# Last feed forward: the second batch's normalized rows made on GpSimd and turned ahead of its low-rank products

## What is computed

```python
h = layernorm(x) * (1 + cb) + sb
logits = h @ gate_w.T + gate_b                  # 8 experts
top_v, top_i = top_k(softmax(logits), 2)
for e in range(8):
    gate = (top_i == e).sum(-1) * top_v.sum(-1)
    inter = h @ wi.T + bi + (h @ lora_A[e].T) @ lora_B[e].T   # 512 wide, rank 16
    out += gate * (relu(inter) @ wo.T + bo)
x = x + gb * out
```

## Time and profile before

| | us |
|---|---|
| median of 3 runs | 973.53 (973.2 to 974.91) |
| the profiled execution | 973.75 |
| its span, first to last instruction | 972.0 |
| TensorE busy | 909.9 (94%) |
| ScalarE busy | 642.2 (66%) |
| VectorE busy | 593.1 (61%) |
| GpSimd busy | 292.5 (30%) |

### The profile page before, as it was taken

How to read it: one execution, slowest core, us unless ns; L and a number is a source line. 1 busy time by engine, 2 the same in 40 slices (tenths; PEclk the granted TensorE clock), 3 DMA queues, 4 the chain that set the end, 5 groups by cost and what they waited for, 6 DMA issues and landing times. The chain is left out here.

```text
span 972.0 us, 25390 instructions
## 1 busy us (share of the span) xinstructions
PE 909.9 (94%) x10211; PEld 668.2 (69%) x10211; DVE 593.1 (61%) x1355; ACT 642.2 (66%) x1094; POOL 292.5 (30%) x367
## 2 busy tenths in 40 slices
PE   7998897369999999999999999999999999998987
PEld 6676576146777767777776777777677777776776
DVE  5556111566666666666666666666666666677975
ACT  2552143158787878778787878778787877884442
POOL 5124800503224242422324142232414223215110
PEclk9998799569999999999999999999999999999999
DMA  8300701100020002002000200100020010000000
GB/s 251 137 2 22 254 26 52 40 1 2 2 90 3 2 2 92 2 2 84 9 3 1 91 2 2 76 17 2 2 91 1 3 31 10 3 1 2 1 23 22
DMA packets 27128, 35.48 MB, mean 37 GB/s; under 512 B 6042, under 2 KB 21716, under 8 KB 26836
## 3 DMA queue, kind: packets, MB, share of 16 engines
q1 hardware_dynamic: 25988, 31.76, 10.0%
q0 software_dynamic: 1024, 2.10, 0.7%
HBM read 28.48 MB, written 5.37 MB: 35 GB/s over the span
## 5 line engine op out<-in xcount | busy, mean ns | idle before, releaser
L552 DVE CUSTOM_DVE_ANT_0 soft<-SC,strips 128x1024 f32<-128x1024 f32 x256 | 303.3, 1223 | 79.7 <-PE SC L394 79.6
L513 ACT ACTIVATE soft<-soft,nmax 128x1024 f32<-128x1024 f32 x256 | 294.1, 1150 | 3.5 <-DVE nmax L552 3.4
L430 PE MATMUL CX<-PTs,V 128*64 128x256 f32 x2048 | 244.7, 381 | 0.0
L498 ACT COPY PTs<-PT 128x1024 f32<-128x1024 f32 x128 | 129.6, 1013 | 139.2 <-PE PT L413 139.2
L394 PE MATMUL SC<-qk 64*128 64x512 f32 x1536 | 212.5, 409 | 7.0 <-DVE nmax L552 6.9
L413 PEld LDWEIGHTS PT<-ident,soft 64*128 64x128 f32 x4096 | 159.0, 139 | 70.2 <-issue 28.9
L430 PEld LDWEIGHTS CX<-PTs,V 128*64 128x64 f32 x2048 | 142.6, 137 | 92.8 <-issue 35.0
L560 DVE COPY PTs<-PT 128x512 f32<-128x512 f32 x128 | 88.5, 692 | 161.0 <-PE PT L413 161.0
L413 PE MATMUL PT<-ident,soft 64*128 64x64 f32 x4096 | 176.4, 226 | 3.9 <-ACT PTs L505 2.4
L394 PEld LDWEIGHTS SC<-qk 64*128 64x128 f32 x1536 | 137.8, 188 | 32.9 <-issue 5.2
L341 POOL CAST qk<-raw_qk 128x512 fp32r<-128x512 f32 x60 | 36.8, 614 | 262.3 <-ACT raw_qk L317 262.3
(11 more groups left out here) (268 smaller groups left out, 998.2 us busy)
## 6 DMA issues: line engine op xcount, KB each, us to landing
strips<-bias_vec SPq DMA_DIRECT2D x8, 1920.0 KB, 7.0
arena<-in_L_ffn_w SPq DMA_DIRECT2D x1, 2048.0 KB, 11.3
slots_in<-arena SPq DMA_DIRECT2D x1, 1536.0 KB, 9.3
arena<-slots_in SPq DMA_DIRECT2D x8, 192.0 KB, 4.5
slots_out<-arena SPq DMA_DIRECT2D x8, 192.0 KB, 2.0
x<-in_L_attn_x SPq DMA_DIRECT2D x2, 512.0 KB, 4.4
out<-x SPq DMA_DIRECT2D x4, 256.0 KB, 2.3
arena<-in_L_wmod SPq DMA_DIRECT2D x2, 384.0 KB, 4.8
```

The source lines that it names most:

```text
L430: ins = pe.matmul(CX[hd * DK:(hd + 1) * DK, 0:2 * P], V1[:, vb, t, hd * DK:(hd + 1) * DK], PTs[:, g % 2, hd, t, :], start=(t == 0), stop=( ...
L498: act.copy(turned_out(n, 0), turned_in(0)).then_inc(ev("ptA_out"), 1)
L513: act.activation(soft[:, n % RING, hd, :], soft[:, n % RING, hd, :], ACT.Exp, bias=nmax[:, j:j + 1], scale=-1.0, accum_out=rsum[:, hd, n % ...
L552: dve.tensor_tensor_reduce(soft[:, n % RING, hd, :], SC[hd][:, :], strips[:, u // B % 2, hd, i * P:i * P + S], 1.0, 3.4e38, ALU.add, ALU.m ...
```

## The change

It touches all four compute engines. VectorE no longer makes batch two's inverse roots and rows, nor waits for var_ready. GpSimd makes them, after split_rows(1) and ahead of split_rows(2): it waits for var_ready, runs its `inverse_roots(tiles(1))`, waits for their end and makes the eight rows with one tensor_scalar each (subtract the mean, multiply by the inverse root, both taken from a column), with the same two signals of h_ready. On TensorE both turns now stand directly behind base(1), ahead of lora(1, 0); they stood between lora(1, 0) and lora(1, 1). On ScalarE the copies of the turned rows stand ahead of both relu groups of part one; they stood between them.

```diff
--- before.py
+++ after.py
@@ -799,6 +799,13 @@
                     split_rows(0)
                 if n == TILES + 1:
                     split_rows(1)
+            pool.wait_ge(ev("var_ready"), batches_until(3, 1))
+            inverse_roots(tiles(1))
+            pool.wait_ge(ev("inverse_ready"), 3)
+            for t in range(TB, NT):
+                ins = pool.tensor_scalar(h[:, t, :], x[:, t, :], mv[:, t, 0:1], st[:, 5, t:t + 1], ALU.subtract, ALU.mult)
+                if t % 4 == 3:
+                    ins.then_inc(ev("h_ready"), 1)
             for k in range(2, 4):
                 split_rows(k)
 
@@ -954,8 +961,8 @@
             relu_out(0, 0)
             relu_out(0, 1)
             low_out(1)
+            norm_out(3, (1,))
             relu_out(1, 0)
-            norm_out(3, (1,))
             relu_out(1, 1)
             router_exp(3, tiles(1))
             for k in range(2, 4):
@@ -1329,11 +1336,8 @@
             spread(1)
             hidden_sums(0)
             norm_stats(3, (1,))
-            dve.wait_ge(ev("var_ready"), batches_until(3, 1))
             low_masked(1)
             y_out(0)
-            inverse_roots(tiles(1))
-            rows_out(tiles(1))
             hidden_sums(1)
             router_shift(3, tiles(1), router_logits(MI, TB))
             y_added(0)
@@ -1689,11 +1693,11 @@
             pe.wait_ge(ev("woA_out"), GROUPS)
             y_rows(0)
             base(1)
-            lora(1, 0)
             pe.wait_ge(ev("low_split"), 2)
             turn_rows(3, 2)
             pe.wait_ge(ev("y_out"), 1)
             turn_rows(3, 3)
+            lora(1, 0)
             lora(1, 1)
             router_logits(1, MI)
             y_rows(1)
```

## The result

The changed kernel took 978.54 us in the median of 20 runs, the kernel before 974.54 in 20 runs beside it. The ratio is 1.0043, 95% interval 1.003 to 1.0057: the change costs 4.2 us (2.9 to 5.6). The forecast of 975.2 was too low, and the time lies above the range.

What follows compares the result with a forecast made beforehand. TensorE, busy 94% of the span, was taken as the bound. 973.75 (profiled) + 0.14 (later start less clock gain) + 1.6 (clock fall) = 975.5, less 0.2 for the median, gave about 975.2 us; range 971.8 to 977.2.

Steps and rivals of the forecast that it cites:

- Roots on GpSimd: Batch two's 14 linked steps on GpSimd start at 915.60 and take 4.06 us, done at 919.66.
- Price of a row: Each of the eight GpSimd tensor_scalar rows of 128 columns costs 0.52 us, priced from one-operation rows.
- The upper bound of 0.86: GpSimd row costs at most 0.86 us, the 256-column row's price; the lower bound was VectorE's 0.27.
- the slower rival: Two operations with column scalars cost more on GpSimd; each 0.1 us a row adds 0.8; 975.6 to 977.9, chance 0.25.
- The order on TensorE: Turns ahead of lora(1, 0): TensorE waits for the rows, then 24 low-rank products last 5.68 us in one block.
- +2.84 for the half that lost its place: On TensorE, lora(1, 0) no longer covers roots and rows, which delays y_rows(1) by 2.84 us.
- The forecast's 1.83: y_rows(1) starts 1.83 us later: +2.84 low-rank half, +0.29 second turn, -1.3 closed hole.
- The clock: TensorE's clock falls in the new 4.66 us hole behind base(1), costing 1.6 us; rival that it stays up: 973.7, chance 0.20.
- 1.69 us for y_rows(1)'s own fall: With no hole ahead of it, y_rows(1) runs at the full clock and takes 1.69 us less.
- 0.14 + 1.6: 0.14 us is the later y_rows(1) start less its clock gain; 1.6 us is the clock's fall in the new hole.
- GpSimd's splits no longer meet the additions: The splits end near 928, before hidden_sums(1) on VectorE, whose additions took 4.22 us beside them and 2.73 in hidden_sums(0).
- The router chain's slack: VectorE's router chain starts at 931.95, not 930.07; masks(2) starts at 939.04, so the slack goes without a price.

Runs made afterwards that it cites:

- both kernels with holes filled: Idle TensorE products added in three holes of the changed kernel (1.0029 of the kernel before) and in two holes of the kernel before (0.9984).
- 1.0059: The changed kernel, unaltered, run again 6 times beside its version with three holes filled: 1.0059 of the kernel before (1.004 to 1.0077).
- the order alone: Kernel before with only the change's order on TensorE and ScalarE, roots and rows still on VectorE: ratio 1.0028 (1.0013 to 1.0042).

## Why the prediction was wrong

- **Roots on GpSimd:** right. 4.06 us forecast, 4.03 measured, start 0.09 us after the statistics. VectorE's masked products beside them kept their price, 0.68 us each.
- **Price of a row: the step that failed.** 0.52 forecast, 0.78 measured, 2.07 us over eight rows (b+7.27 to b+9.34 for the second turn). The nearest row of the trace was of the same instruction but with one operation and a constant, and the line through its two sizes gave the price of that form, 0.54 on record. What was not priced is what the change's form adds. The upper bound of 0.86 held, and the slower rival named this mechanism with 0.8 us for each 0.1. It got a chance of 0.25 because I stayed at the middle row, where I had said myself that no row showed the form.
- **The order on TensorE:** right. One block of 24 products behind the second turn, no hole before y_rows(1), +2.84 for the half that lost its place. Measured at the full clock (both kernels with holes filled), y_rows(3) is at b+47.94 for b+44.39, 3.55 us later. The forecast's 1.83 and 2.07 for the rows make 3.9. Most of the 0.35 between lies behind the second turn: the block lasts 5.57 us to the start of the router's products, not 5.68, and these 1.70 to the start of y_rows(1), where the forecast took their 1.84 on record.
- **The clock: mechanism right, size and bookkeeping wrong.** It fell in the new hole, in both profiles of the changed kernel. I priced that at 1.6 us after the fall in y_rows(1). The block took 7.24 and 8.05 us for 5.68, and the second turn 1.09 for 0.63, so y_rows(1) started 1.92 and 2.74 us later than with the holes filled. And I credited 1.69 us for y_rows(1)'s own fall as a sure gain, from one profile. Five profiles of kernels without that fall had one at lora(2) instead, where before had none; four others in which that hole was left open had none there either. In the mean the fillings give 2.9 us in the changed kernel and 1.6 in the one before. That makes the clock 1.3 us dearer after the change, where the forecast had the two nearly cancel (-1.69 + 1.6), but with a standard error of 1.0 it is not shown that it is dearer.
- **The sum:** 3.55 us of places (from the two profiles with the holes filled) and 1.3 of clock make 4.85 over the kernel before, an estimate. The two sets of runs give 4.2 (2.9 to 5.6) and, from 1.0059, 5.7 (3.9 to 7.5). The forecast had 0.14 + 1.6 = 1.74. Of the 2.5 us that it lacks against 4.2, the rows' 2.07 are by far the largest part; what is left over is within the interval, and no run shows it term by term. The 3.55 stands on single profiles. By the means of the times the filled changed kernel is 4.1 us over the filled one before (standard error 0.8, each taken against the kernel before beside it), which agrees. The kernel before was also 1.0 us slower in the larger set of runs (974.54 for 973.53), which no step of mine could give.
- **GpSimd's splits no longer meet the additions:** right, 2.73 us for 4.22. The router chain's slack was used up without a price, as forecast.
- What stays open: how often each hole brings the clock down. The profiles show where it fell in single executions, and only the filled kernels speak for the mean.

## What to carry to other kernels

A step moved to another engine must be priced in its own form: operations, columns or constants. Where the trace has only a simpler form, take the bound nearer to the dear end (here 0.78 between bounds of 0.27 and 0.86), above all where the step has lost its cover and every tenth of a microsecond is paid eight times. A low clock seen in one profile is no gain in hand when its hole closes; look first for the next hole behind it. And the better change stood in the same trace: the hole before y_rows(1) belonged to GpSimd's split of a part that nobody wanted yet, and one wait on GpSimd was worth 2 us.

## What the runs showed of the hardware

- GpSimd's tensor_scalar on 128x128 float32 costs 0.48 us from start to start with one operation and a constant and 0.77 with two operations and two columns; VectorE's takes 0.27 in the latter form.
- In both profiles of the changed kernel the clock fell while TensorE did nothing between base(1) and the block but two turns of 0.63 us at the full clock. It stayed at the lower level about twice as long as in y_rows(1) (0.56 and 0.58 over the eight us from 919, 0.51 and 0.52 over the seven from 924). With the order alone it fell just ahead of the second turn, and the block lost 1.1 us, not 1.6 or 2.4. In the nine filled holes of the five profiles with idle products of 128 columns it stood at 1.00. Three of the nine prove little, all ahead of lora(2): the same kernels without the filling had no fall there either.
- A VectorE subtraction of 128x64 beside a GpSimd subtraction took 1.32 us for 0.23. The Trainium skill (SBUF, Who interferes with whom) calls the shared port pair an exclusive lock, and says that a VectorE instruction with two SBUF inputs contends with a GpSimd instruction that reads SBUF. The rows agree: VectorE's ended at 924.01, when GpSimd's (922.67 + 1.27) had just ended, and GpSimd's cast, with one input, took 1.08 us for 0.61 beside the additions.
